# Norms moved from GpSimd to VectorE, paired head outputs, fewer whole items and filler products in a fused convolution-attention-recurrence kernel

## The chip, the cores and the metric

One core of one Trainium2 chip runs the whole program. The metric is the time on the device in microseconds; a profiled execution gives a span (first to last instruction) and its own time beside it.

## The reference, cut to what matters

```python
x = conv_attention(x)        # 4 x 64 channels x 1024 positions; softmax over 1024 keys, residual
t = to_tokens(x)             # 4 x 1024 tokens x 64
t = t + causal_attention(ln(t), Wq, Wk, Wv, Wo)     # 8 heads of 64; scores / 8; softmax; sum over heads
t = t + recurrence(ln(t), W, V, gamma, beta)        # Wx, batch norm, y = sigmoid(wx_t + V y_(t-1))
out = from_tokens(t)
# ln(v) = (v - mean) / sqrt(var + 1e-5) over the 64 channels of a token
```

## The kernel before, in words

The work is cut into *items*: 128 keys by 512 queries of scores. The convolution part has 4 batches of 16 items, one a *slot* (slots 0 to 63). Attention has 16 *units*, each a batch and a pair of heads (r is 0 or 1). A unit has 9 items for each head; both heads' items go as a *pair*, so that a unit takes 18 slots, and slots of odd number are empty of items. Below, pair 0 to pair 8 are the pairs of a unit; the unit n begins at slot 64 + 18n.

For every item TensorE makes scores in one of three banks (ST), and ScalarE writes exp(scores) twice, as float32 (`probs`, L775) and as float16 (`probs_high`, L779). GpSimd subtracts them to `probs_low` (L1250, `pool_low`), and TensorE multiplies the values by the high and the low part, three float16 products a tile (L574, L576, L578), four tiles an item. An item that is *whole* (`whole(i)`, the last of every `ATTN_WHOLE` items) skips L779 and L1250: TensorE multiplies in float32 instead (L570, `values<-probs`). The product of an item comes six slots, so three pairs, after its scores (`LAG`).

Everything else is put into slots by hand. Every engine runs the same list of slots in order, and in each slot its own steps in a fixed order. In a slot TensorE does the values of the earlier pair, auxiliary products (queries, values, keys), masks and the *maxes* (L497: a float16 estimate of the scores of a later unit, in two banks MX), and then the scores. VectorE does first `dve_scale` where a half of the outputs closes, then the row maxima of the maxes (L903), the low parts of auxiliary products (L959, L964), then `dve_norms`. TensorE can't write the next maxes until L903 has read the last ones. ScalarE does the auxiliary casts and then the items.

A *half* is 512 queries of one head: its outputs gather in a bank (OT), with the sum of the probabilities in column 65. `dve_scale` takes the reciprocal (L979), multiplies (L983) into `scaled`, a ring of 4, and GpSimd adds it to the tokens (L1260, `pool_add`). Each unit closes its first two halves at pair 5 and the last two at pair 2 of the next unit. TensorE may open a bank again once it is scaled (`s_scaled`).

Norms of the first kind (before attention): VectorE gathers statistics of a batch or a group (`LN1_GROUPS`) and a first guess of the reciprocal root (`rsqrt_start`, L988); GpSimd does three Newton steps of four instructions (L1271 to L1274), subtracts the mean and multiplies (L1286, L1288), sets a column to 1 and copies (L1290, L1291). TensorE transposes that into the keys at `KEY_SLOTS`. Norms of the second kind (before the recurrence) have their Newton steps on GpSimd as well for three of four batches. The tail, after the last item, is a chain: last norm, transposes, products with W, batch norm, then sweeps of the recurrence.

## Time and profile before

| what | us |
|---|---|
| median of 3 runs | 570.09 (568.32 to 572.07) |
| profiled execution, its own time | 568.85 |
| its span | 567.0 |
| busy: PE, ACT, POOL, DVE | 490.0, 429.3, 424.4, 398.8 |

PE is TensorE, PEld its weight loads, DVE is VectorE, ACT is ScalarE, POOL is GpSimd. No engine is busy throughout; the ends of matmuls are modelled, so PE's busy time overstates its load. The time is read as a repeated cycle of 16 attention units, with disturbed units among them.

### The profile page before, as it was taken

The numbers are of one execution on the slowest core, as the hardware profiler recorded it, in microseconds if no ns is written. First come the engines' busy times: TensorE is split into PE (matmuls) and PEld (weight loads), VectorE is DVE, ScalarE is ACT, GpSimd is POOL, SyncE is SP. The second block draws the span as 40 slices with busy tenths as digits, with TensorE's granted clock in tenths as the row PEclk, the third lists the DMA queues.
The fourth block names the chain that finished last, engine by engine and source line by source line (L and its number), as shares of the span: only waits on it lengthen the run. The fifth ranks groups of instructions, "written<-read, shape, count | busy, mean of one in ns | idle before, by whom it ended". The sixth has DMA issues, their size and how long they took to land.

```text
span 567.0 us, 16744 instructions
## 1 busy us (share of the span) xinstructions
PE 490.0 (86%) x6771; PEld 323.0 (57%) x6771; DVE 398.8 (70%) x909; ACT 429.3 (76%) x832; POOL 424.4 (75%) x463
## 2 busy tenths in 40 slices
PE   4699978988799998889999988998999999787783
PEld 1277655655565755565666756565666766564431
DVE  5878888767678786576767676766767786328757
ACT  3488867866778878587888878787888878785593
POOL 3867965857988797968788797899788799985002
PEclk9999999989999999799999999999999999998698
DMA  9100000000000000000000000000000000000001
GB/s 230 68 3 2 2 20 1 4 1 3 1 22 2 3 3 2 3 1 21 2 3 2 4 3 1 21 3 1 1 3 3 2 3 2 2 2 2 0 2 74
DMA packets 3580, 7.46 MB, mean 13 GB/s; under 512 B 1168, under 2 KB 1456, under 8 KB 3376
## 3 DMA queue, kind: packets, MB, share of 16 engines
q1 hardware_dynamic: 3056, 5.34, 3.5%
q8 instruction: 54, 0.88, 0.7%
q10 hardware_dynamic: 448, 1.05, 0.6%
q14 instruction: 22, 0.18, 0.1%
HBM read 4.22 MB, written 1.05 MB: 9 GB/s over the span
## 4 chain that ended last, share of the span: by engine, by line
PE 45%; DVE 22%; POOL 17%; ACT 9%; issue 6%; DMA 1%; DVEq 0%; SPq 0%; POOLq 0%; ACTq 0%
POOL probs_low L1250 10%; PE bank L537 9%; DVE attn_partial_max L903 7%; ACT probs_high L779 6%; PE bank L497 6%; PE bank L570 5%; PE bank L574 4%; DVE conv_partial_max L897 3%; PE bank L578 3%; PE bank L576 3%; PE bank L455 2%; PE bank L522 2%; PE bank L483 2%; PE bank L456 2%; POOL tokens L1260 2%
## 5 line engine op out<-in xcount | busy, mean ns | idle before, releaser
L1250 POOL TENSOR_TENSOR probs_low<-probs,probs_high 128x512 f16<-128x512 f32 x288 | 327.6, 1158 | 77.5 <-ACT probs_high L779 76.7
L775 ACT ACTIVATE probs<-bank 128x512 f32<-128x512 f32 x352 | 214.7, 611 | 84.2 <-PE bank L537 69.0
L903 DVE TENSOR_REDUCE attn_partial_max<-bank 128x1 f32<-128x512 f32 (+2 forms) x288 | 185.3, 685 | 99.5 <-PE bank L497 99.0
L779 ACT ACTIVATE probs_high<-bank 128x512 f16<-128x512 f32 x288 | 176.8, 614 | 0.0
L574 PEld LDWEIGHTS bank<-values_high,probs_high 128*128 128x128 f16 x1152 | 105.7, 98 | 74.2 <-issue 35.8
L574 PE MATMUL bank<-values_high,probs_high 128*128 128x65 f16 x1152 | 128.8, 196 | 15.5 <-POOL probs_low L1250 11.4
L576 PE MATMUL bank<-values_low,probs_high 128*128 128x64 f16 x1152 | 127.6, 194 | 0.0
L578 PE MATMUL bank<-values_high,probs_low 128*128 128x65 f16 x1152 | 127.1, 194 | 0.0
L576 PEld LDWEIGHTS bank<-values_low,probs_high 128*128 128x128 f16 x1152 | 106.9, 99 | 3.2
L578 PEld LDWEIGHTS bank<-values_high,probs_low 128*128 128x128 f16 x1152 | 107.2, 98 | 0.0
L570 PE MATMUL bank<-values,probs 128*128 128x65 f32 x512 | 71.7, 278 | 0.8 <-POOL probs_low L1250 0.8
L570 PEld LDWEIGHTS bank<-values,probs 128*128 128x128 f32 x512 | 64.7, 192 | 3.5 <-POOL probs_low L1250 1.0
L497 PE MATMUL bank<-attn_keys_high,queries_high 64*128 64x512 f16 (+3 forms) x384 | 56.7, 332 | 7.9 <-ACT probs_high L779 6.0
L1260 POOL TENSOR_TENSOR tokens<-scaled_outputs,tokens 128x256 f32<-128x256 f32 x71 | 51.7, 729 | 8.0 <-DVE scaled_outputs L983 3.3
L537 PE MATMUL bank<-queries_high,attn_keys_high 64*128 64x512 f16 (+3 forms) x384 | 55.6, 326 | 1.1 <-ACT probs_high L779 1.1
L537 PE MATMUL bank<-queries_high,attn_keys_low 64*128 64x512 f16 (+3 forms) x384 | 55.5, 325 | 0.0
L537 PE MATMUL bank<-queries_low,attn_keys_high 64*128 64x512 f16 (+3 forms) x384 | 55.5, 325 | 0.0
L897 DVE TENSOR_REDUCE conv_partial_max<-bank 128x1 f32<-128x512 f32 x64 | 42.8, 687 | 5.8 <-PE bank L470 4.7
L983 DVE TENSOR_TENSOR scaled_outputs<-bank,reciprocal_denominators 128x256 f32<-128x256 f32 x72 | 30.6, 425 | 7.6 <-DVE reciprocal_denominators L979 0.5
L522 PE MATMUL bank<-causal_masks,identity_bf 128*128 128x128 bf16 x256 | 27.5, 219 | 6.6 <-ACT probs_high L779 6.4
L497 PEld LDWEIGHTS bank<-attn_keys_high,queries_high 64*128 64x128 f16 x384 | 15.3, 93 | 29.7 <-issue 6.8
L1343 POOL TENSOR_TENSOR x_split<-probs 128x512 f32<-128x512 f32 x4 | 4.2, 1092 | 36.1 <-ACT probs L878 36.1
(192 smaller groups left out, 708.9 us busy)
## 6 DMA issues: line engine op xcount, KB each, us to landing
x_channels<-in_x_cm SPq DMA_DIRECT2D x6, 256.0 KB, 7.6
tokens<-in_x_tm SPq DMA_DIRECT2D x1, 1024.0 KB, 10.4
out<-ln_channels SPq DMA_DIRECT2D x4, 256.0 KB, 2.0
attn_weights<-in_attn_w ACTq DMA_DIRECT2D x1, 512.0 KB, 6.2
attn_keys_split<-attn_keys_high SPq DMA_DIRECT2D x4, 128.0 KB, 2.3
attn_keys_split<-attn_keys_low SPq DMA_DIRECT2D x4, 128.0 KB, 2.4
queries_high<-minus_max_rows SPq DMA_DIRECT2D x32, 2.0 KB
x_channels<-in_x_cm ACTq DMA_DIRECT2D x2, 128.0 KB, 3.2
```

The source lines that it names most:

```text
L497: last[r] = nc.tensor.matmul(prep_bank(m + r)[:, at * P:(at + tiles) * P], q[rows(r), t * P:(t + 1) * P], xs_hi[rows(r), b * N + j0 * P:b ...
L537: last[r] = nc.tensor.matmul(ST[(i + r) % ST_RING][:, at * P:(at + tiles) * P], keys[rows(r), b * N + j * P:b * N + (j + 1) * P], queries[ ...
L570: ins = nc.tensor.matmul(dst, e32[:, item % E_RING, cols], v32[v % 2][:, j, r, :], start=opens, stop=True, skip_group_check=True)
L574: nc.tensor.matmul(dst, hi, v_hi[v % 2][:, j, r, :], start=opens, stop=False, skip_group_check=True)
L576: nc.tensor.matmul(dst[:, 0:C], hi, v_lo[v % 2][:, j, r, :], start=False, stop=False, skip_group_check=True)
L578: ins = nc.tensor.matmul(dst, lo, v_hi[v % 2][:, j, r, :], start=False, stop=True, skip_group_check=True)
L775: ins = nc.scalar.activation(e32[:, i % E_RING, :], o[:], ACT.Exp, scale=scale)
L779: ins = nc.scalar.activation(p_hi[:, i % P_RING, :], o[:], ACT.Exp, scale=scale)
L897: nc.vector.reduce_max(cmx[v % 2][:, t, part:part + 1], o[:], AX).then_inc(s_prep_used, 1)
L903: nc.vector.reduce_max(dst, o[:].rearrange("p (n w) -> p n w", n=n), AX).then_inc(s_prep_used, 1)
L1250: nc.gpsimd.tensor_tensor(out=p_lo[:, i % P_RING, :], in0=e32[:, i % E_RING, :], in1=p_hi[:, i % P_RING, :], op=ALU.subtract).then_inc(s_r ...
L1260: nc.gpsimd.tensor_tensor(out=dst, in0=scaled[:, half % S_RING, :, :], in1=dst, op=ALU.add).then_inc(s_added, 1)
```

## The change

- `ATTN_WHOLE` goes from 6 to 9: two items of a unit are whole (the first head's of pair 4, the second head's of pair 8), before three (the second head's of pairs 2, 5 and 8).
- GpSimd's Newton steps (both kinds of norm) and its normalizing go to VectorE: three instructions a Newton step, one step a slot after `LN1_START_SLOT` (slots 23 to 25, 76 to 78, 130 to 132) and after slots 237 and 309; the normalizing as two tiles at a time over four slots (`dve_ln1_apply`), one instruction a tile that writes both copies.
- Both heads' outputs of a half are scaled by one instruction of twice the size, and VectorE adds the two (`dve_scale_pair`); GpSimd adds once where it added twice. The two output banks become neighbours.
- Filler products (`pe_keep_clock`, 57 of 256 columns) stand ahead of five waits of the tail.

```diff
-CONV_WHOLE, ATTN_WHOLE = 4, 6
+CONV_WHOLE, ATTN_WHOLE = 4, 9
-LN1_APPLY_SLOT = (23, 80, 136, 214)
-KEY_SLOTS = ((32, 34), (88, 92), (154, 160), (226, 232))
+LN1_APPLY_SLOT = (26, 82, 138, 212)
+LN1_APPLY_PACE = (1, 2, 2, 2)
+KEY_SLOTS = ((32, 34), (92, 96), (154, 160), (226, 232))
+def added_by(half):
+    return half + 1 if half < B * NC else B * NC + (half - B * NC) // 2 + 1
-        banks = [... for i in range(8)]
+        banks = [... for i in range(6)]
+        both = ctx.enter_context(nc.psum_tensor("output_banks", [P, 2, CW], f32))
+        def pe_keep_clock(bank, n):
+            for _ in range(n):
+                nc.tensor.matmul(bank[:, 0:2 * P], identbf[:], masks[:].rearrange("p a c -> p (a c)"),
+                                 start=True, stop=True)
             pe.wait_ge(s_l3t, 2)
+            pe_keep_clock(MX[0], 8)
             pe.wait_ge(s_l3, 3)
             pe_transposes(MX[1], xh3, 2).then_inc(s_tr, 1)
+            pe_keep_clock(MX[0], 6)
             pe.wait_ge(s_trc, 1)
             nc.tensor.matmul(ST[0][:], ffn_w[:, 0, :], xh3T[:, 2 * CW:3 * CW], ...)
+            pe_keep_clock(MX[0], 22)
...
             pe.wait_ge(s_aux_used, len(AUXES))
+            pe_keep_clock(ST[1], 3)
...
             pe.wait_ge(s_t2c, 2)
+            pe_keep_clock(MX[0], 18)
+        def dve_scale_pair(half):
+            nc.vector.wait_ge(s_values, CLOSED_BY[half + 1][3] + 1)
+            i = half % S_RING
+            po = both[:, :, 0:TPC * PO].rearrange("p r (t c) -> p r t c", c=PO)
+            nc.vector.reciprocal(rden[:, i:i + 2, :], po[:, :, :, C:PO]...).then_inc(s_recip, 2)
...
+            nc.vector.tensor_tensor(out=scaled[:, i:i + 2, :, :], in0=po[:, :, :, 0:C],
+                                    in1=rden[:, i:i + 2, :]..., op=ALU.mult).then_inc(s_scaled, 2)
+            nc.vector.wait_ge(s_scaled, half + 2)
+            nc.vector.tensor_tensor(out=scaled[:, i, :, :], in0=scaled[:, i, :, :],
+                                    in1=scaled[:, i + 1, :, :], op=ALU.add).then_inc(s_paired, 1)
+        def dve_ln1_apply(b, part):
+            if b and part == 0:
+                nc.vector.wait_ge(s_aux, AUX_OF["keys", 2 * b - 1] + 1)
+            for t in (2 * part, 2 * part + 1):
+                n = b * NT + t
+                ins = nc.vector.tensor_scalar(xh[:, t, :, :], tok[...].unsqueeze(1).to_broadcast([P, 2, C]),
+                                              mv1[:, n, 0:1], rstd1[:, n:n + 1], ALU.subtract, ALU.mult)
+            if part == NT // 2 - 1:
+                link(ins)
+                nc.vector.memset(xh[:, :, :, 0:1], 1.0).then_inc(s_xt, 1)
+                if 0 < g - LN1_START_SLOT[group] <= 3:
+                    dve_newton(rstd1[:, cols], var1[:, cols], nwt1[:, cols])
+            for b in range(B):
+                part, odd = divmod(g - LN1_APPLY_SLOT[b], LN1_APPLY_PACE[b])
+                if 0 <= part < NT // 2 and not odd:
+                    dve_ln1_apply(b, part)
-                    rsqrt_start(r, v).then_inc(s_rstd3, 1)
+                if 0 <= g - slot <= 3:
+                    ln3_rstd(g - slot, b0, b1, ready=s_rstd3)
-        def pool_newton(r, v, w):
-            for _ in range(3): (four linked instructions)
-        def pool_ln1(b):
-            (wait, pool_newton, subtract, multiply, memset, copy)
-                    if half < HALVES - 1:
+                    if half < B * NC or half % 2 == 0 and half < HALVES - 2:
                         pool_add(half)
```

## Rows read from the trace of the kernel before

**Rows 1.** The page: busy time by engine, and the chain's shares.
```profile
PE 490.0 (86%) x6771; PEld 323.0 (57%) x6771; DVE 398.8 (70%) x909; ACT 429.3 (76%) x832; POOL 424.4 (75%) x463
...
PE 45%; DVE 22%; POOL 17%; ACT 9%; issue 6%; DMA 1%; DVEq 0%; SPq 0%; POOLq 0%; ACTq 0%
```

**Rows 2.** Timeline of ACT: start, duration, what, idle before and its releaser.
```profile
217.14 0.60 ACT L775 ACTIVATE probs<-bank 128x512 f32<-128x512 f32 x1 [0.93 <-PE bank L537]
...
246.63 0.60 ACT L775 ACTIVATE probs<-bank 128x512 f32<-128x512 f32 x1 [0.48 <-PE bank L537]
...
294.11 0.60 ACT L775 ACTIVATE probs<-bank 128x512 f32<-128x512 f32 x1 [0.21 <-PE bank L537]
...
296.61 0.60 ACT L775 ACTIVATE probs<-bank 128x512 f32<-128x512 f32 x1 [0.93 <-PE bank L537]
...
309.39 0.60 ACT L775 ACTIVATE probs<-bank 128x512 f32<-128x512 f32 x1
...
312.11 0.60 ACT L775 ACTIVATE probs<-bank 128x512 f32<-128x512 f32 x1 [1.14 <-PE bank L537]
...
314.54 0.60 ACT L775 ACTIVATE probs<-bank 128x512 f32<-128x512 f32 x1 [0.37 <-PE bank L537]
...
320.30 0.60 ACT L775 ACTIVATE probs<-bank 128x512 f32<-128x512 f32 x1 [0.93 <-PE bank L537]
...
346.28 0.60 ACT L775 ACTIVATE probs<-bank 128x512 f32<-128x512 f32 x1 [0.48 <-PE bank L537]
```

**Rows 3.** Groups of the page: count, busy us, mean ns, idle before.
```profile
L1250 POOL TENSOR_TENSOR probs_low<-probs,probs_high 128x512 f16<-128x512 f32 x288 | 327.6, 1158 | 77.5 <-ACT probs_high L779 76.7
...
L1260 POOL TENSOR_TENSOR tokens<-scaled_outputs,tokens 128x256 f32<-128x256 f32 x71 | 51.7, 729 | 8.0 <-DVE scaled_outputs L983 3.3
...
L983 DVE TENSOR_TENSOR scaled_outputs<-bank,reciprocal_denominators 128x256 f32<-128x256 f32 x72 | 30.6, 425 | 7.6 <-DVE reciprocal_denominators L979 0.5
```

**Rows 4.** The chain from 267 to 292 us: start, duration, what.
```profile
267.55 0.03 PE bank L578
267.58 0.92 PE bank L570 x8
```

**Rows 5.** Timeline of POOL around the third norm of the first kind.
```profile
220.53 0.23 POOL L1271 TENSOR_TENSOR newton_scratch<-ln_rstd,ln_var_eps 128x16 f32<-128x16 f32 x1
...
227.12 2.27 POOL L1250 TENSOR_TENSOR probs_low<-probs,probs_high 128x512 f16<-128x512 f32 x2
```

**Rows 6.** Timeline of POOL late in the last unit.
```profile
511.37 6.73 POOL L1250 TENSOR_TENSOR probs_low<-probs,probs_high 128x512 f16<-128x512 f32 x6
```

**Rows 7.** Timeline of DVE: two small steps in that stretch, one earlier, and a chain in unit 7.
```profile
131.70 1.01 DVE L988 TENSOR_SCALAR ln_rstd<-ln_var_eps 128x8 int32<-128x8 int32 x1
...
306.37 1.29 DVE L903 TENSOR_REDUCE attn_partial_max<-bank 128x1 f32<-128x512 f32 x2 [1.00 <-PE bank L497]
...
309.41 1.28 DVE L903 TENSOR_REDUCE attn_partial_max<-bank 128x1 f32<-128x512 f32 x2
...
514.82 1.08 DVE L994 TENSOR_TENSOR ln_newton_scratch<-ln_rstd,ln_var_eps 128x4 f32<-128x4 f32 x1
...
518.16 0.17 DVE L994 TENSOR_TENSOR ln_newton_scratch<-ln_rstd,ln_var_eps 128x4 f32<-128x4 f32 x1
```

**Rows 8.** All instructions of one line: minimum, median, maximum ns.
```profile
L1135 DVE TENSOR_SCALAR ln_tokens<-tokens,ln_mean_var,ln_rstd x4: 305/306/314, 525.4 to 526.1; 128x64 f32<-128x64 f32 x4
```

**Rows 9.** Stretches: length, busy of PE, PEld, DVE, ACT, POOL, then granted clock.
```profile
40.00:60.00 20.00, 18.32 (x241) 13.64 (x239) 17.46 (x47) 17.24 (x34) 15.28 (x25) 1.00 0.01 3
...
525.00:528.00 3.00, 2.06 (x6) 1.56 (x7) 2.43 (x13) 0.77 (x2) 0.00 (x0) 0.50 0.00 0
```

**Rows 10.** Timeline of the tail, PE and ACT.
```profile
527.08 2.04 PE L711 MATMUL bank<-ln_channels,ffn_weights 128*128 128x256 f32 x4
...
536.53 9.91 ACT L870 ACTIVATE y_fp<-bank 128x512 f16<-128x512 f32 x20
...
555.19 3.60 PE L752 MATMUL bank<-probs,ffn_weights 128*128 128x512 f32 x8
```

More of the change, by code:

```diff
@@ L324, in build @@
         outt = xh3T
-        banks = [ctx.enter_context(nc.psum_tensor(f"bank{i}", [P, CW], f32)) for i in range(8)]
-        ST, MX, OT, AUX = banks[0:3], banks[3:5], banks[5:7], banks[7]
+        banks = [ctx.enter_context(nc.psum_tensor(f"bank{i}", [P, CW], f32)) for i in range(6)]
+        both = ctx.enter_context(nc.psum_tensor("output_banks", [P, 2, CW], f32))
+        ST, MX, OT, AUX = banks[0:3], banks[3:5], (both[:, 0, :], both[:, 1, :]), banks[5]
         LN_BANKS, WX_BANKS, BN_BANK = (MX[0], OT[1]), (ST[2], AUX), OT[0]
@@ L370, in build @@
         s_scaled = sem("outputs_scaled")
+        s_paired = sem("outputs_of_both_heads_added")
         s_added = sem("outputs_added")
@@ L980, in dve_scale @@
             if half >= S_RING:
-                nc.vector.wait_ge(s_added, half - S_RING + 1)
+                nc.vector.wait_ge(s_added, added_by(half - S_RING))
             nc.vector.wait_ge(s_recip, half + 1)
@@ L1055, in dve_norms @@
             for slot, b0, b1 in ((LN3_PAIR_SLOT, 0, 2), (LN3_THIRD_SLOT, 2, 3)):
[L1056 to L1059 removed]
+                if 0 <= g - slot <= 3:
+                    ln3_rstd(g - slot, b0, b1, ready=s_rstd3)
             if g == LAST_STATS_SLOT:
[L1061 removed]
+                nc.vector.wait_ge(s_added, added_by(half_of(UNITS - 1, 0, 1)))
                 last_stats(0)
@@ L1102, in _ @@
                 for half in HALVES_AT.get(g, ()):
-                    dve_scale(half)
+                    if half < B * NC:
+                        dve_scale(half)
+                    elif half % 2 == 0:
+                        dve_scale_pair(half)
                 for m in auxes_at(g):
@@ L1123, in _ @@
                 dve_norms(g)
-            dve.wait_ge(s_added, HALVES - 1)
-            dve.wait_ge(s_scaled, HALVES)
+            dve.wait_ge(s_added, added_by(HALVES - 3))
+            dve.wait_ge(s_paired, (HALVES - B * NC) // 2)
             dst = tok3[:, TPC:NT, (B - 1) * C:B * C]
-            link(nc.vector.tensor_tensor(out=dst, in0=scaled[:, (HALVES - 1) % S_RING, :, :], in1=dst, op=ALU.add))
+            link(nc.vector.tensor_tensor(out=dst, in0=scaled[:, (HALVES - 2) % S_RING, :, :], in1=dst, op=ALU.add))
             last_stats(1)
@@ L1255, in pool_add @@
             b = batch_of(v)
-            nc.gpsimd.wait_ge(s_scaled, half + 1)
+            if half < B * NC:
+                nc.gpsimd.wait_ge(s_scaled, half + 1)
+            else:
+                nc.gpsimd.wait_ge(s_paired, (half - B * NC) // 2 + 1)
             if half:
-                nc.gpsimd.wait_ge(s_added, half)
+                nc.gpsimd.wait_ge(s_added, added_by(half) - 1)
             dst = tok3[:, c * TPC:(c + 1) * TPC, b * C:(b + 1) * C]
@@ L1324, in _ @@
                         pool_low(i)
-                for b in range(B):
-                    if g == LN1_APPLY_SLOT[b]:
-                        pool_ln1(b)
                 for n, slot in enumerate((LN3_PAIR_SLOT, LN3_THIRD_SLOT)):
-                    if g == slot + 4:
+                    if g == slot + 8:
                         pool.wait_ge(s_rstd3, n + 1)
-                        v, r, w = ln3_views(2 * n, 2 + n, 0, NT)
-                        pool_newton(r, v, w)
-                    if g == slot + 8:
-                        pool.wait_ge(s_added, (B + (2 + n) * H) * NC)
+                        pool.wait_ge(s_added, added_by((B + (2 + n) * H) * NC - 1))
                 for k in range(NC):
```

45 lines of the change are left out of this document (16 added, 29 removed).

## The prediction

> **What bounds the kernel now.** I read the page first: no engine is busy more than 86% of the span and the chain that ended last runs through four engines, PE 45%, DVE 22%, POOL 17%, ACT 9% [rows 1]. So no single sum of busy time gives the answer, and I went to the start of each pair's first activation on ACT, which paces attention. Unit 7 runs from 296.61 to 320.30, 23.69 us [rows 2]; that is a clean unit. Unit 4 takes 246.63 - 217.14 = 29.49 us and unit 8 takes 346.28 - 320.30 = 25.98 [rows 2]: disturbed by something that is not in the others. Unit 4 holds the third norm on POOL, which keeps POOL from `probs_low` for 227.12 - 220.53 = 6.6 us [rows 5].
>
> Inside a clean unit I ask which wait ends last. ACT idles 0.93 us before pair 0 and 1.14 before pair 6, each ended by PE's scores [rows 2]: these places are bound by PE, or by what PE waits for. One of these is DVE: in unit 7 it works without a pause from the maxes of pair 4 at 306.37 to the end of those of pair 5, 309.41 + 1.28 = 310.69 [rows 7], and PE may not write the maxes of pair 6 before that, while ACT starts pair 6 at 312.11 after its longest wait [rows 2]. So between pairs 4 and 6 every addition to DVE should cost one for one; elsewhere DVE has gaps.
>
> **One item of nine whole.** 16 items more are split. Each costs POOL 1.16 us [rows 3] and ACT about half a us (429.3 us over 832 instructions [rows 1]), and saves PE 0.92 - 12 x 0.03 = 0.56 us: a whole item's products take 0.92 us, and one float16 product of the twelve takes 0.03 [rows 4]. PE gets lighter, then, and the others heavier. Where in the unit it falls decides. The float32 products of pairs 2 and 5 go (read at pairs 5, 6 and 8), those of pair 4 come (read at pair 7). Pair 4's first item gets shorter on ACT, but pair 6 is held by the DVE chain above, so the most I count there is -0.1. Pair 6 to pair 7 is 314.54 - 312.11 = 2.43 and PE-bound, so +0.56. Pair 7 to pair 8 is 294.11 + 23.69 - 314.54 = 3.26, less 0.56 would be 2.70, but ACT has six activations there, some 3.0: -0.3. Together +0.1 to +0.2 in a clean unit; I take +0.1. It may be -0.6 if all saved PE time counts.
>
> **Both heads' outputs by VectorE.** POOL is spared one of two additions of 0.73 us, 32 times, so 23 us against the 18.5 that 16 more `probs_low` cost [rows 3]. It was not the bound of a clean unit, so nothing there. DVE's sum is even: two multiplications of 0.425 [rows 3] become one of twice the columns, some 0.7, and an addition that has the old multiplication's form and so some 0.4; one of two reciprocals and its gap of 0.1 go. PE may open the bank about 0.3 later, and the scores of that slot cover it.
>
> The new thing is the addition's wait. A step of 128x4 on DVE takes 0.17 us at 518.16, when POOL's six subtractions have ended at 511.37 + 6.73 = 518.10, and 1.08 at 514.82, in their midst [rows 6, 7]. In attention the same shows at 131.70: 1.01 us for 128x8. DVE stood until POOL's current instruction, 1.16 long, was over. L983 never shows it: of 72 the mean is 425, and one input comes from PSUM. The pair's addition reads SBUF twice, as L994 does, and so can wait up to 1.1. In the closing at pair 5 it lies in DVE's closed chain. No row shows an addition of this size in POOL's work: its wait is between 0 and 1.1. I take 0.5, about the middle, since the new order leaves POOL with one item of pair 4 at just that time. The closing at pair 2 has a gap behind it. A clean unit thus becomes 0.1 + 0.5 = 0.6 longer; 14 units have maxes beside them: **+8.4** (0 to +17).
>
> The Trainium skill ("SBUF — State Buffer", section "Who interferes with whom") says that a VectorE instruction with two SBUF inputs contends with a GpSimd instruction that reads SBUF, as an exclusive lock for the whole instruction, and that one with a single SBUF input outside the two-port modes doesn't. By that rule the addition and the Newton products wait, the maxes and the scaling don't; it speaks against this change, and it says too that GpSimd stands still behind DVE, which no row here shows. A rule without such a lock would give the first rival below. What follows doesn't rest on this paragraph.
>
> **Newton steps on DVE.** Four groups lie in attention (slots 76 to 78, 130 to 132, and those behind 237 and 309), with nine instructions each. Each takes 0.17 to 1.1 us [rows 7], with the 0.03 of a link between, so 1.8 to 10 us a group. All fall at pairs 6 and 7. DVE has some 2 us of slack there before PE asks for its banks: I read that from its gaps beside a PE-bound pace. POOL works through most of it; about four of the first six wait for it at about 1 us and two are quick, so a little over 4 us come before the maxes of pair 7, and 2.1 us over the slack. When PE stalls for that, POOL runs dry and the rest is quick: the cost limits itself. **4 x 2.1 = +8.4** (0 to +20).
>
> **Normalizing on DVE, in attention.** Three batches of four parts, two instructions each. The nearest row is 0.306 for 128x64 with the same operands [rows 8]; at 128x128 some 0.35. That is 0.7 a part, and with waits for POOL 0.7 to 2.9. Pairs 0 to 3 have gaps (1.00 before 306.37 [rows 7]); the parts of slots 144 and 216 fall into the chain at pair 4. I take 0.5, 1.5 and 1.5: **+3.5** (+1 to +10).
>
> **The first batch, in the convolution.** Here DVE is busy 17.46 of 20 us and POOL 15.28 [rows 9]. DVE gets nine Newton steps and eight normalizings, 9 x 0.17 + 8 x 0.35 = 4.3 us without waits; about 2.5 are idle in such a stretch. With half the waits of a us on nine of them I come to 7 and take **+3** over what is idle or overlapped (+1 to +6).
>
> **What POOL gives back.** Unit 4: 29.49 - 23.69 = 5.8, all of it from the block, since POOL then subtracts without a pause behind it. Unit 8: 2.3. The blocks before units' first batches (in the convolution and unit 1) cost less, since a key transposition waits at the same place: 1 each. The two second-kind Newton blocks on POOL are twelve steps like those of rows 5, about 3.6 us each; near the end POOL is the bound [rows 6], with 2 additions less a unit and one subtraction more. I take 4 for both together. Sum **-14.1** (-8 to -18).
>
> **The tail.** The clock granted is 0.50 from 525 to 528 [rows 9], the lower of its two levels (1.2 of 2.4 GHz). There two float32 products of 256 columns (two records each) take 2.04 us; later four of 512 columns take 3.60, 0.9 for one, which has the same columns as those two [rows 10]: -1.1. The transposes of 128 columns around them and the averaging product give some 0.2 to 0.6 more, if the fillers hold the clock. Their own cost: eight of 256 columns, some 0.9, stand before the first transposes, which may start 0.2 later. In the sweeps ACT runs twenty activations in 9.91 us without a gap from 536.53 [rows 10], so a faster PE gives nothing. **-1.3** (-3 to +1).
>
> **The sum.** 8.4 + 8.4 + 3.5 + 3 - 14.1 - 1.3 = +7.9 us on the profiled execution's 568.85, that is 576.8, with 1.85 around the span as before. The median shown is 1.24 above that execution, which gives **578.0**.
>
> **Rivals.** (a) *POOL's relief wins.* The gaps of POOL meet DVE's steps, and the waits are near nothing: 0.17 us each, all in slack. Then -14.1 - 1.3, clean units 14 x 0.1 = +1.4, the convolution +1: -13, **557**. For it: POOL idles 77.5 us before L1250 [rows 3]; the two steps of 1 us were met by chance or in the closing stretch. Against it: linked steps each come again just as POOL starts its next instruction. (b) *Half of it:* the pair's addition is free (clean units stay at +0.1), the Newton steps cost what I say, the convolution +3 and the parts +2: -13 + 8.4 + 2 + 2 = -0.6, **569.5**, no change. Deciding is whether the addition in the closing of pair 5 meets a subtraction. (c) *The clock falls.* PE stalls behind each Newton group until the clock drops, and the work after it runs at half rate; unit 4 shows what a long stall does. With 2 us more for each of four groups: +8, **586**. It decides once these stalls become as long as the one in unit 4. That POOL remains as loaded as before (18.5 against 23 us plus the norms) is excluded by the counts.
>
> **Chances.** The forecast .38 (572 to 584), (a) .25 (554 to 564), (b) .25 (564 to 573), (c) .12 (584 to 595). The range 559 to 588 leaves out the lower part of (a) and the upper of (c), some 2 in 10. A measurement of this kernel tells 1% (5.7 us) from no change. Under 564.4: (a) and the edge of (b), .27. Within 1%, up to 575.8: the rest of (b) and the forecast's lower end, .28. Slower: .45. Both signs hold much; the likeliest case alone is 572 to 584.
>
> **What would show it.** In the profile after: the addition of two halves with a spread from 0.42 to 1.5 us, and the clean unit 24.2 to 24.8 between starts of pair 0; if it is 23.7 or less, the step "+0.5 for the addition's wait" is wrong. Newton products in attention with a mean near 0.8; if under 0.3, (a). Unit 4 without its 29.49 and no half clock in it; if it stays, POOL was not its cause. Behind slots 78 and 132 a pair interval 2 us longer. L1250's total near 346 us, L1260's near 28, L711 near 1.1. The prediction fails above all if POOL's phase against DVE shifts, since both the addition and the Newton steps hang on that.

## The result, and where the 32.4 us lie

The changed kernel takes 599.69 us in the median of 4 runs (596.21 to 601.26), the kernel before 570.31 beside it (568.32 to 572.07). The ratio is 1.0508, with a 95% interval of 1.0448 to 1.0568. The direction was forecast, the size was not: +7.9 us stood in the sum, and the profiled executions differ by 32.4 (spans 567.0 and 599.4). The medians differ by 29.4, so some 3 us of the 32.4 belong to these two executions; the last section says where they lie.

The page of the changed kernel, busy time and the chain's shares, to be held against [rows 1]:

```profile
PE 490.5 (82%) x6892; PEld 322.9 (54%) x6892; DVE 458.3 (76%) x958; ACT 436.1 (73%) x848; POOL 398.4 (66%) x371
...
PE 40%; DVE 35%; ACT 11%; POOL 8%; issue 4%; DMA 1%; DVEq 0%; SPq 0%; ACTq 0%; POOLq 0%
```

PE is as busy as before, and POOL is spared 26 us. DVE has 59.5 us more, over 49 more instructions, and its share of the chain goes from 22% to 35% while POOL's falls from 17% to 8%. So the chain moved from POOL's stretches onto DVE's. The counted loads came out as the diff says, in the groups of the page (against [rows 3]):

```profile
L1306 POOL TENSOR_TENSOR probs_low<-probs,probs_high 128x512 f16<-128x512 f32 x304 | 347.3, 1160 | 130.5 <-ACT probs_high L799 130.1
...
L1319 POOL TENSOR_TENSOR tokens<-scaled_outputs,tokens 128x256 f32<-128x256 f32 x39 | 28.2, 724 | 13.7 <-DVE scaled_outputs L1009 13.4
```

POOL's idle time ahead of its subtractions rises from 77.5 to 130.5 us. It is waited for less than before, though not never: the tail below has three such waits.

Next, the two starts of pair 0 that bound unit 7, in the timeline of ACT (against [rows 2]):

```profile
314.95 0.60 ACT L795 ACTIVATE probs<-bank 128x512 f32<-128x512 f32 x1 [0.93 <-PE bank L552]
...
340.38 0.60 ACT L795 ACTIVATE probs<-bank 128x512 f32<-128x512 f32 x1 [0.93 <-PE bank L552]
```

The clean unit now takes 25.43 us instead of 23.69, 1.74 more. Read the same way through the whole trace, the difference of the spans falls apart into these pieces (before, then after, us):

| stretch | before | after | difference |
|---|---|---|---|
| start to the first item | 22.7 | 23.3 | +0.6 |
| items 0 to 7 of the convolution | 10.4 | 12.2 | +1.8 |
| items 24 to 31 of the convolution | 12.1 | 17.9 | +5.7 |
| the other 48 items | 66.8 | 66.8 | 0.0 |
| units 0 to 13, 14 clean excesses of 1.74 | | | +24.4 |
| units 0 to 13, all else | | | -0.5 |
| unit 14, and unit 15 up to its pair 8 | 43.1 | 40.8 | -2.3 |
| from the start of pair 8 of unit 15 to the end | 52.0 | 54.7 | +2.7 |

The "all else" hides several large numbers: the four Newton groups (+1.8 us each in units 3, 9 and 13, measured against like units beside them; in unit 0 pair 6 is 2.4 longer than a clean one, but the granted clock is at its lower level from about 139 to 145 us there), what POOL gives back, and 1.3 us that the kernel before lost in unit 0 of this execution alone. The 24.4 are the excess of a clean unit times fourteen. That is a way of counting, not what the addition costs: a unit that is held up by something else need not pay the 1.74 as well. The experiments show how far the two are apart: freeing the addition in the changed kernel gives back 1.07%, some 6 us (e11), and the norms alone cost 3.3%, some 19 us (e3).

**The addition.** Here are DVE's closings in unit 7, at pair 2 and at pair 5, in the timeline of the changed kernel (start, length, what, idle before):

```profile
318.21 0.68 DVE L979 TENSOR_TENSOR values_low<-bank,values_high 128x512 f16<-128x512 f32 x1
319.12 0.21 DVE L1000 RECIPROCAL reciprocal_denominators<-output_banks 128x8 f32<-128x8 f32 x1 [0.23 <-PE output_banks L585]
319.46 0.69 DVE L1005 TENSOR_TENSOR scaled_outputs<-output_banks,reciprocal_denominators 128x512 f32<-128x512 f32 x1
320.19 1.42 DVE L1009 TENSOR_TENSOR scaled_outputs<-scaled_outputs 128x256 f32<-128x256 f32 x1
321.53 1.28 DVE L923 TENSOR_REDUCE attn_partial_max<-bank 128x1 f32<-128x512 f32 x2
...
328.46 1.04 DVE L1009 TENSOR_TENSOR scaled_outputs<-scaled_outputs 128x256 f32<-128x256 f32 x1
```

And POOL at the same two moments:

```profile
319.05 2.27 POOL L1306 TENSOR_TENSOR probs_low<-probs,probs_high 128x512 f16<-128x512 f32 x2 [0.67 <-ACT probs_high L799]
...
328.07 1.16 POOL L1306 TENSOR_TENSOR probs_low<-probs,probs_high 128x512 f16<-128x512 f32 x1 [0.67 <-ACT probs_high L799]
```

The same addition needs 0.42 us when nothing stands against it. At 320.19 it lasts 1.42 and at 328.46 it lasts 1.04, both times with a subtraction under way on POOL. The maxes queue behind it on DVE, then PE's next maxes, the scores behind them and ACT behind those. Over all of the kernel (minimum, median, maximum in ns):

```profile
L1005 DVE TENSOR_TENSOR scaled_outputs<-output_banks,reciprocal_denominators x32: 692/692/693, 135.8 to 551.5; 128x512 f32<-128x512 f32 x32
L1009 DVE TENSOR_TENSOR scaled_outputs<-scaled_outputs x32: 424/882/1422, 136.6 to 552.2; 128x256 f32<-128x256 f32 x32
```

The multiplication, with one input in PSUM, has no spread. The addition, with both in SBUF, has a spread of one us.

**The convolution.** Nine Newton steps and eight normalizings fall into items 24 to 31. DVE's timeline there:

```profile
58.26 1.11 DVE L1028 TENSOR_TENSOR newton_scratch<-ln_rstd,ln_var_eps 128x8 f32<-128x8 f32 x1
59.41 0.17 DVE L1029 SCALAR_TENSOR_TENSOR newton_scratch<-newton_scratch,ln_rstd 128x8 f32<-128x8 f32 x1
59.61 1.03 DVE L1030 SCALAR_TENSOR_TENSOR ln_rstd<-newton_scratch,ln_rstd 128x8 f32<-128x8 f32 x1
...
64.34 0.71 DVE L1056 TENSOR_SCALAR ln_out<-tokens,ln_mean_var,ln_rstd 128x128 f32<-128x128 f32 x2
```

Only two of the nine products wait. But DVE has no gap between 57.66 and 67.7 us, and PE waits behind it. Three stretches of the changed kernel (length, busy of PE, PEld, DVE, ACT, POOL, then the granted clock):

```profile
57.00:62.00 5.00, 2.91 (x32) 2.36 (x32) 4.73 (x14) 2.56 (x5) 2.36 (x3) 1.00 0.00 0
62.00:67.00 5.00, 2.52 (x36) 1.88 (x35) 4.83 (x15) 1.83 (x4) 1.15 (x1) 1.00 0.00 0
67.00:70.40 3.40, 3.40 (x26) 2.28 (x26) 2.44 (x7) 2.13 (x5) 1.83 (x2) 0.50 0.00 0
```

DVE is busy 9.56 of the ten us from 57 to 67, PE 5.43. Before, the same items kept PE busy 10.88 of 12.10 us, and DVE 10.25. From 67.0 the granted clock is at its lower level (1.2 of 2.4 GHz) for 3.4 us.

**The tail.** PE's timeline, with the fillers (L461):

```profile
549.09 1.95 PE L585 MATMUL output_banks<-values,probs 128*128 128x65 f32 x8
550.83 1.91 PE L461 MATMUL bank<-causal_masks,identity_bf 128*128 128x256 bf16 x8
...
555.74 2.56 PE L461 MATMUL bank<-causal_masks,identity_bf 128*128 128x256 bf16 x22
558.14 0.38 PE L599 MATMUL bank<-constants,ln_tokens 128*128 128x128 f32 x2
...
558.99 1.13 PE L730 MATMUL bank<-ln_channels,ffn_weights 128*128 128x256 f32 x4
```

and what the transposes at 558.14 waited for before, the last norm on DVE:

```profile
556.49 0.98 DVE L1191 TENSOR_SCALAR ln_tokens<-tokens,ln_mean_var,ln_rstd 128x64 f32<-128x64 f32 x4
```

The clock was up where the fillers were meant to hold it: L730 takes 1.13 us where L711 took 2.04 [rows 10]. But in this execution it fell earlier, at 548.3, after PE had waited for POOL's last subtractions (three waits of 0.57 to 0.58 us from 545.6 to 548.4). These waits don't explain the fall by themselves: e4 and e11 below have waits of the same lengths at the same place, and there the clock stays up. The float32 products and the first eight fillers ran at the lower level (1.95 and 1.91 us; in e4 below, at the upper one, 1.08 and 1.04), which is 1.7 us. The 22 fillers behind them ended at 558.3, when all four steps of the norm had been over since 557.47. So the transposes started some 0.7 us later than the norm allowed, behind the work that was to speed them up. And the clock fell again at 585.8, so that the first four of the last eight products, which took 3.60 us in all before [rows 10], take 3.45 by themselves:

```profile
586.07 3.45 PE L772 MATMUL bank<-probs,ffn_weights 128*128 128x512 f32 x4
589.35 1.88 PE L772 MATMUL output_banks<-probs,ffn_weights 128*128 128x512 f32 x4
```

That is 1.6 us more (591.23 - 586.07 = 5.16).

How much of the +2.7 is the fillers' doing is settled by e11, whose tail has the same code. Its clock stays up from the last pair's start until 575.6 us, late in the sweeps, its first eight fillers take 1.04 us, and its transposes wait for the norm and not for the fillers:

```profile
544.37 2.57 PE L460 MATMUL bank<-causal_masks,identity_bf 128*128 128x256 bf16 x22
547.58 0.55 PE L598 MATMUL bank<-constants,ln_tokens 128*128 128x128 f32 x2 [0.64 <-DVE ln_tokens L1190]
```

From the start of pair 8 of unit 15 to the end e11 takes 51.8 us, against 54.7 in the changed kernel and 52.0 before. The 2.7 us thus come with the clock's fall at 548.3, which one of two executions of the same tail has; without it the fillers neither cost nor give much.

### The profile page after: what moved, and what is told of

It reads as the page before. It is cut to its first block, busy times and chain, and to the rows that moved or that the text cites. A ratio compares the mean times of both kernels' runs of the same rounds, so it can differ in the third digit from the quotient of the medians.

```text
span 599.4 us, 16927 instructions
## 1 busy us (share of the span) xinstructions
PE 490.5 (82%) x6892; PEld 322.9 (54%) x6892; DVE 458.3 (76%) x958; ACT 436.1 (73%) x848; POOL 398.4 (66%) x371
## 4 chain that ended last, share of the span: by engine, by line
PE 40%; DVE 35%; ACT 11%; POOL 8%; issue 4%; DMA 1%; DVEq 0%; SPq 0%; ACTq 0%; POOLq 0%
DVE attn_partial_max L923 11%; PE bank L552 7%; POOL probs_low L1306 7%; ACT probs_high L799 6%; PE bank L512 5%; PE output_banks L585 5%; DVE conv_partial_max L917 4%; PE output_banks L589 3%; ACT probs L795 3%; DVE queries_low L984 2%; DVE ln_out L1056 2%; PE output_banks L593 2%; DVE scaled_outputs L1009 2%; PE output_banks L591 2%; DVE scaled_outputs L1005 2%
## 5 line engine op out<-in xcount | busy, mean ns | idle before, releaser
L1306 POOL TENSOR_TENSOR probs_low<-probs,probs_high 128x512 f16<-128x512 f32 x304 | 347.3, 1160 | 130.5 <-ACT probs_high L799 130.1
L589 PEld LDWEIGHTS output_banks<-values_high,probs_high 128*128 128x128 f16 x1216 | 112.3, 99 | 64.4 <-issue 37.9
L589 PE MATMUL output_banks<-values_high,probs_high 128*128 128x65 f16 x1216 | 133.1, 197 | 13.2 <-DVE scaled_outputs L1005 8.2
L591 PE MATMUL output_banks<-values_low,probs_high 128*128 128x64 f16 x1216 | 132.1, 194 | 0.0
L593 PE MATMUL output_banks<-values_high,probs_low 128*128 128x65 f16 x1216 | 131.7, 195 | 0.0
L591 PEld LDWEIGHTS output_banks<-values_low,probs_high 128*128 128x128 f16 x1216 | 113.1, 99 | 3.7 <-issue 0.5
L593 PEld LDWEIGHTS output_banks<-values_high,probs_low 128*128 128x128 f16 x1216 | 113.2, 98 | 0.0
L585 PEld LDWEIGHTS output_banks<-values,probs 128*128 128x128 f32 x384 | 49.6, 198 | 10.1 <-issue 7.6
L585 PE MATMUL output_banks<-values,probs 128*128 128x65 f32 x384 | 53.5, 284 | 0.0
L498 PE MATMUL bank<-causal_masks,identity_bf 128*128 128x128 bf16 x251 | 27.5, 221 | 18.2 <-DVE attn_partial_max L923 18.2
L1319 POOL TENSOR_TENSOR tokens<-scaled_outputs,tokens 128x256 f32<-128x256 f32 x39 | 28.2, 724 | 13.7 <-DVE scaled_outputs L1009 13.4
L537 PE MATMUL bank<-causal_masks,identity_bf 128*128 128x128 bf16 x256 | 27.5, 220 | 8.6 <-ACT probs_high L799 8.5
```

Source lines behind the costliest of these rows:

```text
L585: ins = nc.tensor.matmul(dst, e32[:, item % E_RING, cols], v32[v % 2][:, j, r, :], start=opens, stop=True, skip_group_check=True)
L589: nc.tensor.matmul(dst, hi, v_hi[v % 2][:, j, r, :], start=opens, stop=False, skip_group_check=True)
L591: nc.tensor.matmul(dst[:, 0:C], hi, v_lo[v % 2][:, j, r, :], start=False, stop=False, skip_group_check=True)
L593: ins = nc.tensor.matmul(dst, lo, v_hi[v % 2][:, j, r, :], start=False, stop=True, skip_group_check=True)
L1306: nc.gpsimd.tensor_tensor(out=p_lo[:, i % P_RING, :], in0=e32[:, i % E_RING, :], in1=p_hi[:, i % P_RING, :], op=ALU.subtract).then_inc(s_r ...
L1319: nc.gpsimd.tensor_tensor(out=dst, in0=scaled[:, half % S_RING, :, :], in1=dst, op=ALU.add).then_inc(s_added, 1)
```

## The experiments

The ratios are all to the kernel before, timed beside each. A clean unit is unit 7, by the starts of its pair 0.

| kernel | what it is | median us | ratio, 95% interval | clean unit |
|---|---|---|---|---|
| e1_whole9 | one item of nine whole | 573.2 | 1.0064 (1.0041 to 1.0086) | 23.76 |
| e2_pair | both heads scaled and added by DVE | 583.3 | 1.0227 (1.0173 to 1.0281) | 24.88 |
| e3_norms | norms and Newton steps on DVE | 589.25 | 1.0327 (1.0274 to 1.0381) | 23.69 |
| e4_fill | fillers in the tail | 568.61 | 0.9985 (0.9965 to 1.0005) | 23.69 |
| e5_pair_psum | e2, one input of the addition in PSUM | 573.82 | 1.0060 (1.0037 to 1.0084) | 24.15 |
| e6_extra_sbuf | before, and 32 unused additions from SBUF | 586.86 | 1.0308 (1.0249 to 1.0366) | 24.42 |
| e7_extra_psum | its twin, one input in PSUM | 577.21 | 1.0121 (1.0083 to 1.0160) | 24.03 |
| e8_spread | norms stay on POOL, cut into steps | 565.95 | 0.9923 (0.9901 to 0.9946) | 23.69 |
| e9_newton | Newton steps alone on DVE | 576.77 | 1.0113 (1.0077 to 1.0148) | 23.69 |
| e10_apply | e8, normalizing alone on DVE | 579.12 | 1.0146 (1.0106 to 1.0185) | 23.69 |
| e11_after_psum | the changed kernel, addition as in e5 | 592.39 | 1.0401 (1.0352 to 1.0451) | 24.03 |
| e12_spread_fill | e8 with the fillers | 563.67 | 0.9877 (0.9832 to 0.9921) | 23.69 |

### The four parts, each by itself

**e1_whole9.**

```diff
-CONV_WHOLE, ATTN_WHOLE = 4, 6
+CONV_WHOLE, ATTN_WHOLE = 4, 9
```

> The kernel before with ATTN_WHOLE = 9 and nothing else. The recorded theory gave the moved items +0.1 us in a clean unit and took the rest of a unit's lengthening (1.74 us, 23.69 to 25.43) for the paired addition: then this is 570 to 573 us, and a clean unit is 23.6 to 23.9. The rival, that the items' places are the main cost (pair 6's interval is 0.4 longer after the change, and more is split for ScalarE and GpSimd), gives clean units of 24.7 or more and 585 us or more.

Measured 1.0064, 573.2 us, a little over the range. The clean unit is 23.76, so +0.07 against the +0.1 of the prediction. But 14 x 0.07 is 1.0 us, and the ratio says 3.6: most of this part's cost lies outside the clean units (unit 1 takes 27.88 us against 27.22, unit 10 28.88 against 27.97, unit 13 24.67 against 24.06). The intervals of its pairs show the trade that was counted: pairs 4 and 7 get shorter (2.26 to 1.95, 3.26 to 2.88), pairs 5 and 6 longer (2.72 to 3.03, 2.43 to 2.82). Within the clean unit the gains and losses nearly cancel.

**e2_pair.** The kernel before with `dve_scale_pair` and the neighbouring output banks, and POOL adding once where it added twice:

```diff
+            nc.vector.tensor_tensor(out=scaled[:, i:i + 2, :, :], in0=po[:, :, :, 0:C],
+                                    in1=rden[:, i:i + 2, :]..., op=ALU.mult).then_inc(s_scaled, 2)
+            nc.vector.tensor_tensor(out=scaled[:, i, :, :], in0=scaled[:, i, :, :], in1=scaled[:, i + 1, :, :],
+                                    op=ALU.add).then_inc(s_paired, 1)
```

> The kernel before with both heads' outputs scaled and added by VectorE (items, norms and tail as before). If the addition's wait for GpSimd's instruction and the wait for both halves' closing carry the unit's lengthening: clean units 25.1 to 25.6 us, in pairs 2 and 5 above all, and 588 to 594 us less what GpSimd's relief gives in disturbed units (some 5), so 583 to 592. If the items carry it: 568 to 573.

Measured 1.0227, within the range. The clean unit is 24.88, +1.19, under the 25.1 to 25.6 that I expected. Pair 2 goes from 2.29 to 3.18 us, pair 5 from 2.72 to 3.01. So three quarters of a clean unit's cost fall on the closing at pair 2, which I had priced at nothing.

**e3_norms.** The kernel before with `dve_ln1_apply` and the Newton steps on DVE, with their slots:

```diff
+                if 0 < g - LN1_START_SLOT[group] <= 3:
+                    dve_newton(rstd1[:, cols], var1[:, cols], nwt1[:, cols])
...
+                part, odd = divmod(g - LN1_APPLY_SLOT[b], LN1_APPLY_PACE[b])
+                if 0 <= part < NT // 2 and not odd:
+                    dve_ln1_apply(b, part)
```

> The kernel before with the norms of the first kind and all Newton steps on VectorE (items, scaling and tail as before). Theory: clean units stay at 23.7; the convolution grows by 7 us (57.0 to 74.9 after the change against 54.6 to 66.7 before), the Newton groups cost 1.8 each and the parts 8, against 14 to 16 given back: 570 to 577 us. Rival: without the other two parts VectorE has room, and this part alone is a gain: 556 to 565.

Measured 1.0327, 589.25 us: the dearest part, and 12 us over the theory, 24 over the rival. Neither held. Clean units stay at 23.69, so none of it is the excess that the changed kernel has in every unit. Items 24 to 31 take 17.7 us, units 1, 3, 9 and 13 take 30.62, 25.78, 30.79 and 27.33 (before 27.23, 24.31, 26.29 and 24.06), and unit 4, which was to be relieved of its 29.48, has 29.59. What POOL gave back in unit 4 was taken again by DVE: in the prediction's terms this part was 8.4 + 3.5 + 3 - 14.1 = +0.8 us, and it cost 18.6 by the ratio.

**e4_fill.** The kernel before with `pe_keep_clock` at its five places.

> The kernel before with the 57 filler products of the tail alone. After the change the stretch from the last pair's start to the end was 54.7 us against 52.0, and the fillers ran past the moment at which the last tokens were ready (some 1.3 us), while they saved some 1.5 us of half clock. Theory: no change within 1 us, 568 to 572. Rival: they are what made the tail longer: 572 to 573.5.

Measured 0.9985, with 1 inside the interval. The fillers alone are neutral within the noise: in this kernel the clock is at its upper level when they start (its 8 first take 1.04 us), and the transposes behind the 22 still wait 0.66 us for DVE, so nothing is held up.

The four ratios add up to 6.0% against the 5.1% of the whole. The whole is not worse than their sum; the parts overlap. Of the 6.0%, 3.3 are the norms', 2.3 the pair's and 0.6 the items', less 0.15 for the fillers.

### Is it the wait for POOL, or DVE's work?

**e5_pair_psum.** e2 with the second head's product left in its PSUM bank, so that the addition has one input in PSUM:

```diff
-            nc.vector.tensor_tensor(out=scaled[:, i:i + 2, :, :], in0=po[:, :, :, 0:C], ...)
-            nc.vector.tensor_tensor(out=scaled[:, i, :, :], in0=scaled[:, i, :, :], in1=scaled[:, i + 1, :, :],
-                                    op=ALU.add).then_inc(s_paired, 1)
+            nc.vector.tensor_tensor(out=po[:, 1, :, 0:C], in0=po[:, 1, :, 0:C], in1=rden[:, i + 1, :]..., op=ALU.mult)
+            link(nc.vector.tensor_tensor(out=scaled[:, i, :, :], in0=po[:, 0, :, 0:C], in1=rden[:, i, :]..., op=ALU.mult))
+            nc.vector.tensor_tensor(out=scaled[:, i, :, :], in0=po[:, 1, :, 0:C], in1=scaled[:, i, :, :],
+                                    op=ALU.add).then_inc(s_scaled, 2)
```

> As e2_pair, but the second head's product is written back to its PSUM bank and the sum reads it there, so that no VectorE instruction of the step has two inputs in SBUF; VectorE has three instructions of 256 columns instead of one of 512 and one of 256. Theory (the addition waits for GpSimd's instruction, 0.6 to 1.0 us of a clean unit's two closings): the sum takes 0.42 everywhere and clean units are 23.9 to 24.3 us, 572 to 577 us in all. Rival (it is the size of VectorE's work and the wait for both halves' closing): clean units stay at 24.9, 583 us.

Measured 1.0060 against e2's 1.0227, the theory and not the rival, though DVE has one instruction more a closing and about the same work. The addition in e2 (ns):

```profile
L996 DVE TENSOR_TENSOR scaled_outputs<-scaled_outputs x32: 425/807/1439, 131.2 to 535.1; 128x256 f32<-128x256 f32 x32
```

and in e5:

```profile
L995 DVE TENSOR_TENSOR scaled_outputs<-output_banks,scaled_outputs x32: 424/425/426, 130.9 to 526.5; 128x256 f32<-128x256 f32 x32
```

Pair 2 is back at 2.29 us: the gap I had claimed behind that closing is there, and it covers the addition, but not a wait of one us. Pair 5 stays longer (3.17), which is the price of waiting for both heads' halves and of the instructions themselves, 0.46 a unit.

**e6_extra_sbuf and e7_extra_psum.** The kernel before with 32 additions more, one a closing, whose result nobody reads. The two differ only in where the first input lies:

```diff
+                nc.vector.tensor_tensor(out=spare[:], in0=cst[:, 0:TPC * C]..., in1=cst[:, TPC * C:2 * TPC * C]..., op=ALU.add)
```
```diff
+                nc.vector.tensor_tensor(out=spare[:], in0=po[:, :, 0:C], in1=cst[:, TPC * C:2 * TPC * C]..., op=ALU.add)
```

> The kernel before with one more addition of 128x256 on VectorE ahead of each second head's scaling (32 in all), both inputs constants in SBUF, its result unused. Theory: it waits up to 1.15 us for GpSimd's instruction where one runs; mean 0.7 to 1.0 us instead of 0.42, clean units 24.8 to 25.5. Rival (no lock, size only): 0.42 each, clean units 24.1 to 24.4, as its twin.

> The twin of e6_extra_sbuf: the same addition at the same place, one input the output bank in PSUM. Both theories: 0.42 us each; 0.34 of it one for one at pair 5 and part of it at pair 2, so clean units 24.0 to 24.4 us, 574 to 580 us in all. The difference to e6_extra_sbuf is the lock's.

The line of the extra addition in e6:

```profile
L985 DVE TENSOR_TENSOR spare_sum<-constants x32: 426/795/1364, 129.0 to 537.0; 128x256 f32<-128x256 f32 x32
```

and in e7:

```profile
L985 DVE TENSOR_TENSOR spare_sum<-bank,constants x32: 425/425/426, 132.6 to 530.3; 128x256 f32<-128x256 f32 x32
```

Same work, same place, same count: 1.0308 against 1.0121. The clean unit of e6 came out at 24.42, under the 24.8 to 25.5 that I had expected, so less of the wait reached the path there than in the pair (0.39 a clean unit, 24.42 less 24.03). The verdict rests on the ratio and the spread, and both are clear: of 17.6 us, 6.9 are the instruction and 10.7 the wait and what it starts.

**e11_after_psum.** The changed kernel with the addition of e5, the same edit.

> The changed kernel with the addition's second input in PSUM as in e5_pair_psum. Clean units of the changed kernel are 25.43 us, 0.55 more than e1_whole9 and e2_pair add up to. If that is the lock too (the new place of the whole item puts a subtraction of GpSimd over the addition): clean units 24.2 to 24.6, 14 times 0.9 less, so 585 to 589 us. If the items' order costs it on TensorE: 24.8 or more, 591 to 594.

Measured 1.0401, so 1.1% of the 5.1% come back. The clean unit goes from 25.43 to 24.03. That would be 1.40 x 14 = 19.6 us, but the span falls only from 599.4 to 588.8. Units 4 and 8 take 31.63 and 30.80 us here, against 28.26 and 29.09 in the changed kernel. In both, pairs 5 and 6 take 5.2 us each (4.4 and 2.8 in the changed kernel's unit 4, 5.2 and 2.9 in its unit 8), and the granted clock falls to its lower level late in pair 5 (at 247.9 and 353.7; in the changed kernel at 357.1 in unit 8, and not in unit 4). So a gain in the clean units met a new loss in the units with normalizing parts. Nor did the other units gain 1.40: units 2, 3, 5 and 9 gain 0.5 to 0.7, units 1 and 10 about nothing, and units 0 to 13 together 5.7. Of the span's remaining difference, 1.8 us lie in items 0 to 7 and 2.9 in the tail, both by the clock and neither by the edit. The expectation of 585 to 589 us was missed for this reason: a clean unit's gain can't be multiplied by fourteen. Why units 4 and 8 lost stays open; no experiment here separates the clock from the order of the waits.

### What moving the norms costs, and what POOL's relief is worth

**e8_spread.** The rival way to relieve POOL: nothing changes engine; the twelve Newton instructions and the four normalizing ones are cut into six steps, one every slot in the convolution and every second slot in attention. The keys of batch 1 go four slots later for it (88 and 92 become 92 and 96).

```diff
-LN1_APPLY_SLOT = (23, 80, 136, 214)
+LN1_STEP_SLOTS = ((23, 24, 25, 26, 27, 28), (76, 78, 80, 82, 84, 86), (130, 132, 134, 136, 138, 140),
+                  (None, None, None, 212, 214, 216))
...
-                    if g == slot + 4:
+                    if g in (slot + 1, slot + 3, slot + 5):
```

> The kernel before with the norms left on GpSimd, but its block cut into six steps (three Newton steps, subtract, multiply, set and copy), one step every other slot (slots 23 to 28, 76 to 86, 130 to 140, 212 to 216; the second kind's Newton steps at 1, 3 and 5 slots behind the start), and the keys of batch 1 at 92 and 96. If unit 4's 5.8 us and unit 8's 2.3 came from one long block on GpSimd, they go: unit 4 at 24 to 25.5 us, 557 to 564 us in all. Rival (GpSimd's load as such, 13 us of it, is what costs): within 3 us of the kernel before.

Measured 0.9923, 4.4 us faster, between the theory's 557 to 564 us and the rival. ACT's starts of units 4 and 5 show it:

```profile
217.68 0.60 ACT L776 ACTIVATE probs<-bank 128x512 f32<-128x512 f32 x1 [0.93 <-PE bank L538]
...
243.65 0.60 ACT L776 ACTIVATE probs<-bank 128x512 f32<-128x512 f32 x1 [0.48 <-PE bank L538]
```

Unit 4 takes 25.97 us instead of 29.48 and unit 1 takes 25.21 instead of 27.23. Unit 4's pair 3 falls from 7.73 to 2.41 us. The block on POOL was the cause of unit 4's length, and most of it fits into gaps once cut. Unit 8, without a Newton step, changes little: 25.69 against 25.98. In unit 1 the later keys of batch 1 may have a share.

**e9_newton.** The kernel before with the Newton steps of both kinds on DVE; normalizing stays on POOL.

> The kernel before with the Newton steps of both kinds on VectorE and the normalizing left on GpSimd (slots 26, 80, 136, 214). e3_norms cost 3.3% (19 us): this run and the next say which half. Theory: 45 linked small instructions, each up to 1.15 us beside GpSimd: +1.5 to +4.5 us in units 3, 9 and 13 as in e3_norms, +2 in the convolution, and 3 us back in unit 4, whose block is half as long: 572 to 579 us.

Measured 1.0113, within the range. Items 24 to 31 of the convolution take 16.1 us against 12.1, so +4.0 where +2 was expected. Unit 4 falls to 24.96, the whole of its excess but 1.3. Unit 3, with a group, has 25.78 (+1.5); units 9 and 13, with the groups of the second kind, 29.91 and 27.12 (+3.6 and +3.1). In these two, pair 7 takes 6.87 and 6.33 us instead of 3.26, and the granted clock falls within it (at 373.4 and 475.8).

**e10_apply.** e8 with the normalizing alone on DVE, in the change's slots.

> As e8_spread, but the normalizing of the first kind on VectorE as in the changed kernel; Newton steps on GpSimd, one a slot. Theory: the 32 instructions take 0.66 us on average instead of 0.35 and lie in VectorE's closed stretches; against e8_spread +3 in the convolution, +3 in unit 1, +4 in unit 4, +2 in unit 8: 574 to 582 us. Rival (the Newton steps were all of it): as e8_spread, 564 to 568.

Measured 1.0146, so 2.2% over e8. ACT's starts of units 4 and 5, and of units 8 and 9:

```profile
227.09 0.60 ACT L778 ACTIVATE probs<-bank 128x512 f32<-128x512 f32 x1 [0.93 <-PE bank L540]
...
257.82 0.60 ACT L778 ACTIVATE probs<-bank 128x512 f32<-128x512 f32 x1 [0.48 <-PE bank L540]
...
331.51 0.60 ACT L778 ACTIVATE probs<-bank 128x512 f32<-128x512 f32 x1 [0.93 <-PE bank L540]
...
360.39 0.60 ACT L778 ACTIVATE probs<-bank 128x512 f32<-128x512 f32 x1 [0.48 <-PE bank L540]
```

30.73 and 28.88 us, so 4.8 and 3.2 over e8, in unit 1 5.6, and in items 24 to 31 of the convolution 17.8 against 12.9, so 5.0. The step itself, and the stretch where it stands worst:

```profile
L1027 DVE TENSOR_SCALAR ln_out<-tokens,ln_mean_var,ln_rstd x32: 331/733/1199, 62.8 to 349.0; 128x128 f32<-128x128 f32 x32
```
```profile
240.00:247.00 7.00, 4.62 (x50) 3.37 (x52) 5.62 (x16) 2.60 (x6) 4.83 (x5) 0.73 0.01 2
```

A batch is eight such steps, 8 x 0.73 = 5.9 us of DVE, by the median, and the units and items with such a batch grow by 3.2 to 5.6 us. DVE is busy 5.62 of 7 us there, while PE has 4.62 and its clock was down for part of the stretch.

### The combination that pays

**e12_spread_fill.** e8 and the fillers of e4, nothing else.

> e8_spread with the fillers of the tail: the two parts that cost nothing or gave something. By e8_spread (0.9923) and e4_fill (0.9985): a ratio of 0.988 to 0.994 to the kernel before, 563 to 567 us. If the fillers' gain was chance: as e8_spread.

Measured 0.9877 (0.9832 to 0.9921), 563.67 us: faster than the kernel before and the changed one, with no step moved to DVE. Its interval and that of e8 (0.9901 to 0.9946) overlap, so that the fillers add something to e8 is not shown.

## Why the prediction was off, step by step

**What bounds the kernel.** Right as far as it was tested: waits added to DVE at pairs 2 and 5 lengthened the clean unit, and cutting POOL's block shortened unit 4. That the same chain sets the length of every disturbed unit is not shown.

**Items moved, "+0.1".** Right for a clean unit (+0.07 in e1); the 3.6 us of the whole of e1 were not in the sum.

**"+0.5 for the addition's wait".** This is the first of two steps that failed, as a term of the sum that was mis-sized: 8.4 us stood there with the items moved. A clean unit's excess times fourteen is 24.4; alone, e1 and e2 cost 2.9%, 16.6 us, with what POOL gives back late in the kernel already off. Two things were off. The size: at pair 5 the wait is 0.62 (1.04 less 0.42), near my 0.5, and with the wait for both heads' halves it comes to +0.3 to +0.8. And the place: "the closing at pair 2 has a gap behind it" was true of an addition of 0.42, as e5 shows with 2.29, and false of one of 1.42, as e2 shows with 3.18. So a second cost of 0.89 a unit was left out. The upper end that I had written for the term, +17, was too low for the clean units' 24.4, because it counted one closing of two. The mechanism is shown from three sides (e2 with e5, e6 with e7, the changed kernel with e11). In the changed kernel 1.40 of the 1.74 a clean unit are the wait; the rest is e1's 0.07 and what else the new closing costs. In the whole kernel the wait is worth less than 14 x 1.40: e11 gives back 1.07%, 6 us.

**The norms, net +0.8.** This is the second step that failed, and by the runs the larger. Newton steps, normalizing and convolution stood at 8.4 + 3.5 + 3 against the whole of what POOL gives back, -14.1; e3 made it 3.27%, 18.6 us. The three paragraphs on its terms below say where. What the norms cost in the changed kernel itself, beside the pair's addition, no run separates.

**The Trainium skill's rule.** The twins answer to the Trainium skill, "SBUF — State Buffer", section "Who interferes with whom", on both sides. Where both inputs lie in SBUF the addition grows by up to nearly one GpSimd instruction of 1160 ns (426 to 1364 ns in e6), and where one lies in PSUM it doesn't (425 to 426 in e7). The same section names `tensor_scalar` among the instructions that can enter a two-port mode and so contend; the normalizing step is one, and its 333 to 1235 ns in the changed kernel agree, though no run here has a twin of it that could show the cause. I had priced it at 0.35 and let "0.7 to 2.9" stand as a range. The rule was weighed and believed; the fault was to take half of its price and to apply it at one closing.

**Newton steps, "4 x 2.1".** Near in the changed kernel: 1.8 in units 3, 9 and 13, and in unit 0 up to 2.4, with the clock down there (e3 and e9 have 1.3 in that unit), so 6.7 to 7.8 against 8.4. The count of waits was not right: the 36 products in attention take 14.9 us, 0.41 each, not 0.8. In e3 and e9, where the pair's addition is absent and pair 7 is the longer of the two, units 9 and 13 lost 3.1 to 4.5 us, with the clock down. That is the mechanism of rival (c), seen in two groups of four in those kernels; in the changed kernel's units 3, 9 and 13 the clock stays up.

**Normalizing, "+3.5", and the convolution, "+3".** Both too low. In the changed kernel items 24 to 31 cost 5.7; against e8's arrangement with 1.74 added, units 1, 4 and 8 cost 3.0, 0.5 and 1.7, so 5.2. In e10 the same parts cost 5.6, 4.8 and 3.2. What fails here is "Pairs 0 to 3 have gaps": unit 1 has its parts there, and it lost most. A likely reading is that a gap on DVE before its maxes is time in which PE works on what DVE released last, so that a step put into it delays the next release; no run tests it. In unit 1 of the changed kernel the clock was also down, from about 166 to 169.4 us.

**"What POOL gives back", -14.1.** Its largest part was right: unit 4's excess vanishes when the block goes (25.97 in e8, 24.96 in e9), and units 10 (its clean excess taken out), 14 and the start of 15 gain 2.7, 1.5 and 0.85, so 5.1 where 4 were said (the last two also in e2, where the norms stay on POOL). In the changed kernel units 1, 4 and 8 together win only 0.6 us, since the parts on DVE take the rest.

**The tail, "-1.3".** Wrong by sign in this execution, +2.7. L730 has its 1.13. The clock was down at 548.3 (+1.7) and again at 585.8 (+1.6), where the step had "if the fillers hold the clock", and the 22 fillers, whose number is fixed, then stood 0.7 us ahead of ready work. With the clock up, the same tail takes 51.8 us in e11, -0.1, and e4's ratio is 0.15% under 1, some 0.9 us, with 1 inside the interval. So -1.3 was too much in either case.

**What is not the change's.** 1.8 us in items 0 to 7, 1.3 the other way in unit 0, and the clock's part of the tail: see the last section.

**The rivals.** (a) and (b) lived on the gaps of POOL meeting DVE's steps; the median addition took 0.88 us, so they met subtractions instead. (c) came true as a mechanism in e3 and e9 and not in the changed kernel's groups, and it stood at 586, since it was built on the forecast's clean unit.

## What to carry to other kernels

Before a step goes to a DVE that is in a closed chain with PE, price it with its longest wait, not the middle, and at every place where it stands: a place that hides the step need not hide the step with its wait. A two-input step whose inputs lie in SBUF can be freed by leaving one input in PSUM, which cost an instruction more and won 1.7% here (e5 against e2). And a block that stalls others is first to be cut into pieces on its own engine: that won 0.8% alone and 1.2% with the fillers, where moving it lost 3.3% (the step from 0.8 to 1.2% is within the noise). And the excess of an undisturbed unit, times the number of units, overstates what a repair gives back: 19.6 us by that count, 6 measured.

## What the runs showed that I had not expected

The granted clock falls at places that differ between executions of the same code. The code up to slot 22 is the same in e8 and e12. Their stretch from 28 to 38 us, e12 and then e8:

```profile
28.00:38.00 10.00, 10.00 (x96) 7.09 (x97) 5.67 (x10) 7.24 (x15) 5.90 (x6) 0.83 0.01 3
```
```profile
28.00:38.00 10.00, 8.58 (x102) 6.52 (x103) 7.11 (x13) 8.32 (x18) 6.76 (x7) 1.00 0.01 3
```

Items 0 to 7 take 12.2 us in e12 and 10.4 in e8. The other twelve traces fall into the same two kinds: 10.4 us where the clock is up in those items (before, e1, e4, e5, e11), 12.2 to 12.3 where it is down for part of them (after, e2, e3, e6, e7, e9, e10). A piece of 1.8 us of a profiled span is thus luck, and a comparison of two spans has to take it out before it explains the rest. It is not the only place. In the trace of the kernel before, pair 2 of unit 0 takes 5.71 us against 4.43 to 4.44 in all thirteen others, with the clock down (length, busy of PE, PEld, DVE, ACT, POOL, then the granted clock):

```profile
121.00:124.00 3.00, 3.00 (x32) 1.53 (x32) 1.25 (x3) 0.00 (x0) 0.60 (x1) 0.53 0.00 0
```

And the tail of the changed kernel takes 2.9 us more than the same code in e11. Together these are 1.8 - 1.3 + 2.9 = 3.4 us of the 32.4, about what separates the profiled executions' difference from the medians' 29.4.

The other surprise is how little of DVE's added time had to wait to do harm. In the convolution two of nine Newton products waited, some 2 us in all, and 5.7 us were lost: the plain work of a full engine, PE idle behind it, and 3.4 us at the lower clock after that. How the 5.7 divide among these no run shows; the Newton steps alone lengthened the same items by 4.0 (e9), the normalizing alone by 5.0 (e10 against e8).
